# Two-layer mixture in seven-product form: the second layer's steps begin one place later in the period

## What is computed

```
s0, s1 = relu(x @ swi[j]) @ swo[j]            # two shared nets, hidden size 2048
eo     = relu(x @ wi[label]) @ wo[label]      # one expert net per batch
w      = softmax(relu([eo, s0, s1][token 0] @ g1) @ g2)
x      = x + eo*w[0] + s0*w[1] + s1*w[2]
x      = x + x @ W[category] + b[category]
```

## Time and profile before

| | |
|---|---|
| median of 3 runs | 2041.92 us (2038.39 to 2043.65) |
| the profiled execution | 2036.01 us |
| its span | 2034.2 us |
| mean granted TensorE clock | 0.989 |
| PE busy | 1956.8 us, 96% of the span, 8504 matmuls |
| VectorE, ScalarE, GpSimd busy | 1269.4, 968.5, 877.3 us |
| DMA queues | 65.3% of 16 engines' span |

### The profile page before, as it was taken

One profiled execution on the slowest core, in us unless ns is written; L12 is line 12 of the kernel. 1 busy time (PEld: TensorE's weight loads), 2 busy tenths in 40 slices (PEclk: granted clock), 3 DMA queues, 4 the chain that ended last, 5 costly groups with the idle time before them and its releaser, 6 DMA issues.

```text
span 2034.2 us, 24901 instructions
## 1 busy us (share of the span) xinstructions
PE 1956.8 (96%) x8504; PEld 1603.7 (79%) x8504; DVE 1269.4 (62%) x1186; ACT 968.5 (48%) x1441; POOL 877.3 (43%) x607
## 2 busy tenths in 40 slices
PE   6999999999899999999999999998989999999998
PEld 5777777777788888888788888887768888888886
DVE  6787788687654565445744554578874655455545
ACT  5655665555553343334443444356544643334342
POOL 5757775677422232233522322366563322223223
PEclk8999999999999999999999999999999999999999
DMA  6657666766676776566686676577568866666653
GB/s 222 228 226 262 257 228 244 298 233 239 229 255 207 223 238 204 180 197 194 209 269 195 194 242 197 198 257 259 227 220 275 256 215 210 208 191 201 196 161 124
DMA packets 187024, 450.98 MB, mean 222 GB/s; under 512 B 16916, under 2 KB 57876, under 8 KB 180500
## 3 DMA queue, kind: packets, MB, share of 16 engines
q1 hardware_dynamic: 186900, 449.39, 65.3%
HBM read 308.81 MB, written 140.51 MB: 221 GB/s over the span
## 4 chain that ended last, share of the span: by engine, by line
PE 79%; DVE 7%; issue 5%; POOL 4%; DMA 3%; ACT 2%; SPq 0%; POOLq 0%; ACTq 0%; DVEq 0%
PE rps L1248 38%; PE ups L1248 37%; PE aps L1248 3%; DMA PDR<-in_L_cond_wo_dram 2%; DVE HL L963 2%; DVE WD L953 1%; POOL HT L609 1%; DVE WU L946 1%; POOL XT L556 1%; DVE ACC L980 1%; DVE XL L937 1%; DVE gacc L1027 0%; POOL XT L659 0%; DMA PDR<-in_L_cond_swo_dram 0%; DMA XT<-in_x_dram 0%
## 5 line engine op out<-in xcount | busy, mean ns | idle before, releaser
L1248 PE MATMUL rps<-HH,WD 128*128 128x512 f32 x2688 | 890.4, 393 | 39.8 <-issue 38.8
L1248 PE MATMUL ups<-XH,WU 128*128 128x512 f32 x2688 | 894.7, 393 | 33.5 <-DVE hid L993 10.0
L609 POOL TENSOR_TENSOR HT<-hid 128x512 f32<-128x512 f32 x192 | 270.0, 1406 | 957.5 <-PE rps L1248 856.3
L1248 PEld LDWEIGHTS rps<-HH,WD 128*128 128x128 f32 x2688 | 509.2, 189 | 155.3 <-issue 47.5
L1248 PEld LDWEIGHTS ups<-XH,WU 128*128 128x128 f32 x2688 | 508.7, 189 | 151.1 <-DVE hid L993 14.2
L1248 PE MATMUL ups<-XL,WU 128*128 128x512 f32 x1344 | 527.0, 392 | 0.0
L1248 PE MATMUL rps<-HL,WD 128*128 128x512 f32 x1344 | 526.7, 392 | 0.0
L963 DVE TENSOR_TENSOR HL<-HT,HH 128x1024 fp32r<-128x1024 f32 x240 | 311.9, 1320 | 50.3 <-POOL HT L609 32.8
L983 DVE SCALAR_TENSOR_TENSOR ACC<-rps,gw,ACC 128x1024 f32<-128x1024 f32 x129 | 165.4, 1282 | 281.9 <-PE rps L1248 281.9
L1248 PEld LDWEIGHTS rps<-HL,WD 128*128 128x128 f32 x1344 | 254.6, 189 | 52.3
L1248 PEld LDWEIGHTS ups<-XL,WU 128*128 128x128 f32 x1344 | 254.6, 189 | 51.9
(11 more groups left out here) (102 smaller groups left out, 1487.2 us busy)
## 6 DMA issues: line engine op xcount, KB each, us to landing
WU<-wu_kept SPq DMA_DIRECT2D x448, 256.0 KB, 3.3
WD<-wd_kept SPq DMA_DIRECT2D x224, 512.0 KB, 3.4
wd_kept<-WD SPq DMA_DIRECT2D x112, 512.0 KB, 3.1
wu_kept<-WU SPq DMA_DIRECT2D x32, 1024.0 KB, 5.8
wu_kept<-WU SPq DMA_DIRECT2D x32, 768.0 KB, 3.3
sums_kept<-ACC SPq DMA_DIRECT2D x28, 512.0 KB, 5.0
MB<-sums_kept SPq DMA_DIRECT2D x28, 512.0 KB, 5.8
PUR<-in_L_cond_swi_dram SPq DMA_DIRECT2D x16, 512.0 KB, 7.0
```

The source lines that it names most:

```text
L609: pool.tensor_tensor(dst, p, q, op).then_inc(s_T, 1)
L1248: ins = pe.matmul(dst, stationary[a], moving[c], start=start and j == 0, stop=stop and j == 2, skip_group_check=True)
```

## The change

Second-layer product (m, i) moves to the place after: place i of period m now holds `down(*place_of(m, i))`, which is product i-1 of step m, and product 6 of step m-1 at place 0. One product, `down(47, 6)`, follows the last period. All engines' orders are rewritten around it:

- `HI_ORDER`, `LO_ORDER`: high parts in the order 0, 1, 3, 2, 6, 4, 5 and low parts 0, 3, 1, 2, 6, 4, 5 (block 6 was before 2 and before 1).
- GpSimd: the last sum of half 0 (`which` 3, it reads the blocks that product 5 of the step before must have left) moves from before the sums of half 1 into them; the sum `which` 2 of half 1 comes after `which` 3. `T_COUNT` gives the new counts. Both `up_sums` of the period now stand between the sums of half 1 and those of the next half 0.
- VectorE and ScalarE: `second(i)` serves `place_of(m, i)`; the low and high parts of block 6 come after `second(0)`; `first_down_product` comes after `relu_11(a)`; `block_21(a)` comes after `second(2)` and after low part 4.
- `made_after`: the operands of step N's second layer are made at the products numbered 0, 1, 2, 4 (two of them), 5 and 6, none at number 3; so the first of a step is made two places later than before.
- `blocks_down` may start before the last low part is made, but waits for all four block sums; GpSimd's `down_sums` gets the wait for the low parts instead.
- SyncE: loads, spills and keeps follow the products that they belong to.

```diff
-HI_ORDER = [0, 1, 6, 2, 3, 4, 5]
-LO_ORDER = [0, 6, 1, 2, 3, 4, 5]
+HI_ORDER = [0, 1, 3, 2, 6, 4, 5]
+LO_ORDER = [0, 3, 1, 2, 6, 4, 5]
+
+T_COUNT = [(1, 2, 3, 6), (4, 5, 8, 7)]
...
+def place_of(m, i):
+
+    return divmod(PRODUCTS * m + i - 1, PRODUCTS)
...
+def made_after(m, i):
+
+
+    e = down_of(m, i) + WD_SLOTS
+    made = {PRODUCTS - WD_SLOTS: [], PRODUCTS - WD_SLOTS + 1: [e - 1, e]}.get(i, [e])
+    return [k for k in made if k >= 0 and prepared(k // PRODUCTS)]
...
                 if PREP[N] >= 1:
-                    sp.wait_ge(s_wld, PRODUCTS * PREP[N])
+                    sp.wait_ge(s_wld, PRODUCTS * PREP[N] - 1)
+                    sp.wait_ge(s_Sd, 4 * PREP[N])
...
                 if d >= 0:
-                    for which in range(4):
-                        hidden_sum(d, 1, which)
+                    hidden_sum(d, 1, 0)
+                    hidden_sum(d, 1, 1)
+                    hidden_sum(d, 0, 3)
+                    hidden_sum(d, 1, 3)
+                    hidden_sum(d, 1, 2)
                 if prepared_half(2 * N + 1):
                     up_sums(2 * N + 1)
+                if prepared_half(2 * N + 2):
+                    up_sums(2 * N + 2)
...
                 if d >= 0:
-                    hidden_low(d, 6)
-                if d >= 0:
+                    hidden_low(d, 3)
                     hidden_low(d, 1)
                     hidden_low(d, 2)
                 if start:
                     token_low(s + 1, 5)
                 second(0)
...
                 if d >= 0:
-                    hidden_low(d, 3)
+                    hidden_low(d, 6)
...
                 second(1)
                 block_22(a)
                 out_part(0, 0)
-                block_21(a)
-                mix(0, 0)
...
                 if d >= 0:
                     hidden_low(d, 4)
                 second(2)
+                block_21(a)
+                mix(0, 0)
...
-                pe.wait_ge(s_hlo, PRODUCTS * N + (1, 3, 4, 5, 6, 7, 7)[i])
+                pe.wait_ge(s_hlo, PRODUCTS * N + LO_ORDER.index(i) + 1)
...
-                    if d >= 0:
-                        down(d, i)
+                    step, which = place_of(m, i)
+                    if step >= 0:
+                        down(step, which)
...
+            down(STEPS - 1, PRODUCTS - 1)
```

More of the change, by code:

```diff
@@ L823, in second @@
                 def second(i):
[L825 to L828 removed]
+                    step, which = place_of(m, i)
+                    if step >= 0:
+                        begin_sum(step, which)
+                    for e in made_after(step, which):
                         down_high(e // PRODUCTS, e % PRODUCTS)
[L831 to L832 removed]
                 if more:
@@ L880, in _ @@
                 second(3)
+                if more:
+                    seventh_product(b)
                 if gating:
@@ L883, in _ @@
                     act.activation(gt[:, :], aps[:, 0:KD], ACT.Relu).then_inc(s_grelu, 1)
+                if more:
+                    chain(b)
                 for ms, c, stage in mixing[1]:
@@ L886, in _ @@
                         mix_high(ms, c)
-                if more:
-                    seventh_product(b)
-                    chain(b)
                 if prepared_half(b + 1):
```

133 lines of the change are left out of this document (63 added, 70 removed).

## The result

The changed kernel takes **2031.60 us** (median of 5, 2030.28 to 2036.04), the kernel before 2039.18 beside it (5, 2037.66 to 2043.65): ratio 0.9961, 95% interval 0.9943 to 0.9978. By the two ratios it is 8 to 11 us faster, where 24 were forecast. The time lies inside the outer range (1993 to 2040 us), but 1.6 us outside the forecast's own bounds (2005 to 2030 us), on the slow side.

A forecast was written before the change was run, and what follows sets the result against it. TensorE was taken to bound most of the time, helpers 16 prepared periods (1 to 11, 31 to 35) that lose 66.1 us. Gains of 24.1 us from 2041.9 gave 2017.8 us; forecast 2005 to 2030 (0.57), outer range 1993 to 2040.

The forecast's parts named there:

- 34 and 35: End of super 2: some 10.5 us still lost there; periods 31 to 35 together gain 7.4 us.
- the beginning: Periods -1 and 0: the pipeline fills a place later, GpSimd starts later on sums: -1.5 us, from -4 to +3.
- The wait at product 1: Prepared periods: product 1, 2.0 to 3.1 us late for low part 1, comes 5.44 us later, so the wait goes.
- (a): Copy of product 0, which product 1 waits for: about 2 us late, given back by low part 6's move; about 0.
- (b): block_22(a), needed by up(a, 6) at place 3: 0 to 1.6 us late, taken as 1.7 us per prepared period.
- Periods 10 and 11: End of super 0: token sums ahead of down_sums, product 1 some 6 us late, clock drop 1.7; gain 3.5 us.
- Period 23: End of super 1: the same as periods 10 and 11 with idle helpers, 1.5 us left; gain 4.0 us.
- The last period: End of the kernel: nothing covers the longer chain to product 1; -0.5 us.
- Mixing periods: Four periods with mixing, one at 680 us: gain 0.7 us each, +2.8 us.
- periods 13, 37: Four scalings of 1.14 us ahead of the copy of product 0, done at 14.4 us, wanted at 13.6: -1.5 us.
- Rival 2: Shared SBUF reads: VectorE and GpSimd exclude each other, prepared periods stay near 40 us; 2038.6 us, chance 0.18.
- Rival 4: Wait at product 1 stays, by the copy of product 0, 2 us per prepared period; 2022.6 us, inside the forecast's 0.57.

The follow-up runs named there:

- low3_late: The change with VectorE's low part 3 moved from the head of the row to behind the addition of product 6: 2032.99 us, ratio 0.9970.
- add_first: The change with the addition of product 6 on VectorE between low parts 3 and 1: 2021.65 us, ratio 0.9898.
- block22: The change with block 22 of prepared periods ahead of two weight low parts and second(1): 2021.26 us, ratio 0.9892.
- both: The change with the edits of add_first and block22 together: 2009.22 us, ratio 0.9829.
- narrow_down: The change with GpSimd's down sums of steps 11 and 35 over a quarter of the columns (sums incomplete): 2025.32 us, ratio 0.9926.
- four: three, with the last token sum of each ending super made by VectorE, not GpSimd: 1996.90 us, 0.9788 of the kernel before.
- token_first: The change with GpSimd's last token sum of an ending super ahead of the down sums: 2032.87 us, ratio 0.9964.
- before_low1b: The kernel before, low part 1 ahead of low part 6, TensorE's count for product 1 two, block 22 waiting for three: 2031.84 us, ratio 0.9964.
- three: both, with block 21 of the second half ahead of two weight low parts on VectorE: 2002.13 us, ratio 0.9813.
- narrow: The change with GpSimd's sums of up weights over a quarter of the columns in most prepared halves (weights left out): 2011.40 us, ratio 0.9858.

## Why the prediction was right in its sign and wrong in its size

18.9 us are missing between the forecast and the table. They lie mainly in four places: 9.1 at the ends of the supers (10 and 11: 2.7; 23: 3.3; 34 and 35: 3.1), 4.8 in periods 1 to 9, 3.7 in the last period, and 1.9 in the periods that hardly wait. 31 to 33 add 0.4, and the beginning came 1.0 better than forecast.

- **The wait at product 1 goes.** The half about low part 1 was right: no row of the change waits there without a releaser, and 38.8 us are gone. What that term left open was (a).
- **Step (a), the copy of product 0, "about 0": a step that failed.** I had 2 us late and took them back, because low part 6 "has left the head of VectorE's row". Low part 3 has come to stand in its place, so that the row has three low parts there in both, and the addition itself moved from ahead of them (336.29 us in the kernel before) to behind them (344.62). Measured 1.24 us in period 7 and 17.9 us in 14 waits, with 4.7 in the last period. low3_late shows it: without low part 3 there the wait in period 7 is 0.25. In the whole span 8.2 us of such waits are left, so low part 3 is not all of it. What this step cost is above all the last period. In periods 1 to 7 it cost nothing by itself, since block 22 comes no sooner without it (add_first).
- **Step (b), `block_22`: 0 to 1.6 us late, taken as 1.7 us a period: right in kind, too small.** Without (a) in front of it the wait is 1.85 us (period 5), or 27.0 / 14 = 1.9 (add_first), and a period loses (282.0 - 266.6) / 7 = 2.2. The row through VectorE from GpSimd's last half-sum that reads `HT` to the block takes 10.7 us in period 7 (339.66 to 350.35), inside the 9.2 to 10.9 counted; GpSimd's sum is through at 7.6 us, where I had 6.9. (The terms that I named, 10.6 + 7.0 - 10.9, make 6.7.) Half a microsecond in each of periods 1 to 7 is 3.5 us.
- **(a) and (b) are neither a sum nor a shadow.** They are two points of one row. Taking away (a) alone moved its loss to (b) (add_first 282.6, low3_late 284.7), taking away (b) alone won 4.0 (block22), both 7.3.
- **Periods 10 and 11: +3.5, measured 0.8; 34 and 35 the same: the step that failed by most.** I put the loss on product 1, some 6 us late (and wrote 11.3 where 6, 1.7 and 2 x 1.7 make 11.1). In period 11 product 1 waits 0.66 us. What waits, 5.97 us, is the first half's product with token part 2, for GpSimd's last token sum. I had written that the four token sums stand ahead of `down_sums`; the last one stands behind them. The shift did win 6.0 us in period 10, and period 11 gave 5.2 back, because this chain came hardly sooner: counted from the start of period 10, the last token sum ends at 50.5 us, before at 51.2. narrow_down shows that less work of GpSimd shortens it, four that a part of it can go to VectorE, and token_first that one other order does not help. That no order of any engine helps is not shown: before_low1b won 2.8 us in these periods.
- **Period 23: +4.0, measured 0.7.** "The same with idle helpers" was unfounded: token and hidden low parts queue on VectorE as in 11, and TensorE waits 2.30 us for token part 5, which stands behind three hidden low parts. four takes 41.0 there for 42.9, before_low1b 41.1.
- **The last period: -0.5, measured -4.2.** Here (a) has no prepared weights to blame: it is the addition behind three low parts, 4.7 us of waiting, with the clock at 0.94 in the first profile. add_first gives 5.9 us back.
- **Mixing periods +2.8 and periods 13, 37 -1.5** came within 0.3 us each of what was said, but four more periods (14, 17, 38, 41) lose 0.4 each before a seventh product.
- **Rival 2, shared reads.** A prepared period isn't bound at 40 us: in three it takes 267.6 / 7 = 38.2 with every sum made. The Trainium skill (SBUF — State Buffer, Who interferes with whom) has the two engines exclude each other; with my 40 us as a floor it would have forbidden that. But my 40 us added listed lengths, and these run into each other: the row after a 0.68 starts 0.60 later (349.67 and 350.27), the one after a 1.21 1.13 later (350.27 and 351.40). With these steps my 18.7 us of VectorE are 7 x 1.13 + 15 x 0.60 = 16.9, and with GpSimd's 21 the two in turn are an estimated 38 us. So the measured 38.2 doesn't speak against the exclusion; whether it is whole isn't settled.
- **Rival 4** is what happened at product 1, at 1.2 us a period where it had 2, and its 2022.6 was too low, since it took everything else as forecast.

How much the shift of the places brought by itself stays open in part. Exchanging two low parts in the kernel before does as much (before_low1b), in other periods. But the 34 us of four were won on top of the change, and I did not try the edits of both, three and four on the kernel before.

## What to carry to other kernels

When an order moves by a place, write the helper's row from the old releaser to each thing that is waited for, before and after, instruction by instruction: an instruction that left the head matters only if none took its place. Two waits on one engine's row can be one shortage: price the later one without the earlier (here in the periods that have no earlier one) before you count on removing either. At the end of a stage ask of each waiting product which helper instruction comes last, not which was late before: what was won in period 10 was lost again in 11. Where a stretch has more helper work than time, move work to an engine that stands idle in it. And a count-based wait names no operand: after an exchange of producers it holds back the wrong consumer.

## What was not expected of the hardware

A `PUS` with a quarter of the columns took 1.30 us beside a low part (VectorE's three run from 325.06 to 330.87) and 0.32 once they were through. With all columns it is 1.71 (341.90 above) and 0.74. GpSimd in narrow:

```profile
328.49 1.30 POOL L586 TENSOR_TENSOR PUS<-PUR 128x64 f32<-128x64 f32 x1
329.75 1.30 POOL L587 TENSOR_TENSOR PUS<-PUR 128x64 f32<-128x64 f32 x1
331.02 0.32 POOL L589 TENSOR_TENSOR PUS<-PUS,PUR 128x64 f32<-128x64 f32 x1
```

So in these two sizes the price of company is not a factor on GpSimd's length but a constant, 0.98 and 0.97 us, most of one low part's 1.21. That fits waiting for one to pass, as the Trainium skill's rule on exclusion (SBUF — State Buffer, Who interferes with whom) says. By these rows small GpSimd operations beside large VectorE ones are the dearest for their size.

The executions of the kernel before spread over 10.6 us in one job (2034.7 to 2045.3), with clocks of 0.989 to 0.982; those of four over 3.0 us (5 executions). That a kernel is steadier because it waits less isn't shown: the change spreads over 5.3 us with waits of about the same total, and before_low1b over 12.3 us.
